# A six-layer decoder pipeline: its pass cut at other places, and the top-k mask moved from ScalarE to GpSimd

## What is computed

```
x = x + attn_latent(ln(x))          # 16 heads of 16, k and v from a latent of 64
x = x + head_mixing(ln(x), ctx)     # per token: 16 heads of 64 attend to each other's heads
x = x + depth_ffn(ln(x))            # router takes the best 128 of 256 tokens, FFN 256-1024-256
x = x + sparse_attn(ln(x))          # softmax over scores that keep their top 25 of 256, others 0
x = x + cross_attn(ln(x), ctx)      # 16 heads of 16, keys beyond a length masked
x = x + ternary_linear(ln(x))
```

## Time and profile before

| | us |
|---|---|
| median of three runs | 6784.98 |
| the profiled execution, its own time | 6756.82 |
| its span from the first to the last instruction | 6755.0 |
| TensorE matmul busy | 5896.7 |
| VectorE busy | 4510.2 |
| ScalarE busy | 4012.6 |
| GpSimd busy | 1507.3 |

### The profile page before, as it was taken

The page is one execution under the profiler, slowest core; times in us unless marked ns, Lnnn a source line. Parts: engine busy times, 40 slices in busy tenths (PEclk is TensorE's granted clock), DMA queues, the critical chain, the costliest instruction groups (busy, mean ns, idle before and its releaser), DMA issues. The chain is left out here.

```text
span 6755.0 us, 109667 instructions
## 1 busy us (share of the span) xinstructions
PE 5896.7 (87%) x37509; PEld 3877.2 (57%) x37762; DVE 4510.2 (67%) x16186; ACT 4012.6 (59%) x9761; POOL 1507.3 (22%) x2564
## 2 busy tenths in 40 slices
PE   6888988988988988898888898888898898898876
PEld 3565565565565565565565565566556556556542
DVE  1366766666777666776676676666776666677653
ACT  2465666565666665666656566656566655566632
POOL 0122222222222222222222222222222222222211
PEclk7789989899999899999999899999998999999965
DMA  2000000000000000000000000000000000000000
GB/s 79 4 6 6 4 8 6 8 8 6 4 8 7 6 8 6 4 8 8 6 8 6 6 6 8 6 8 7 7 4 8 6 8 8 6 4 8 4 2 5
DMA packets 29456, 54.18 MB, mean 8 GB/s; under 512 B 8145, under 2 KB 9810, under 8 KB 27986
## 3 DMA queue, kind: packets, MB, share of 16 engines
q1 hardware_dynamic: 28770, 45.73, 2.1%
HBM read 37.33 MB, written 8.39 MB: 7 GB/s over the span
## 5 line engine op out<-in xcount | busy, mean ns | idle before, releaser
L914 POOL TENSOR_TENSOR t_pr<-t_pr,sc 128x512 f32<-128x512 f32 x512 | 649.6, 1269 | 1495.9 <-ACT t_pr L839 1495.9
L350 DVE TENSOR_REDUCE m_nm<-bankM 128x2 f32<-128x512 f32 x1024 | 657.0, 683 | 347.9 <-PE bankM L340 344.0
L887 DVE MATCH_REPLACE8 wk<-m,wk 128x256 f32<-128x256 f32 x2048 | 821.0, 408 | 0.0
L340 PE MATMUL bankM<-m_kT,m_q 32*128 32x256 f32 x4096 | 698.5, 466 | 75.4 <-DVE m_nm L350 74.3
L883 DVE MAX8 m<-wk 128x8 f32<-128x256 f32 x2048 | 759.2, 412 | 0.0
L651 ACT ACTIVATE xk_area<-bankH,xb 64x256 f32<-64x256 f32 x1024 | 480.7, 469 | 460.4 <-PE bankH L546 438.1
L394 PE MATMUL bankM<-m_q,m_kT 32*128 32x512 f32 x2048 | 627.9, 691 | 0.0
L883 DVE MAX8 m<-sc 128x8 f32<-128x256 f32 x1024 | 380.0, 412 | 327.5 <-ACT sc L830 290.1
L340 PEld LDWEIGHTS bankM<-m_kT,m_q 32*128 32x128 f32 x4096 | 411.3, 216 | 312.4 <-DVE m_nm L350 133.6
L845 ACT ACTIVATE t_pr<-t_pr,t_nm 128x256 f32<-128x256 f32 x1024 | 463.9, 504 | 182.5 <-POOL t_pr L914 180.5
L408 ACT ACTIVATE m_pT<-bankM,keymask 128x512 f32<-128x512 f32 x512 | 323.7, 683 | 247.4 <-PE bankM L394 247.4
(11 more groups left out here) (207 smaller groups left out, 12011.2 us busy)
## 6 DMA issues: line engine op xcount, KB each, us to landing
xin<-x_in SPq DMA_DIRECT2D x32, 256.0 KB, 2.6
ctxA<-ctx_in SPq DMA_DIRECT2D x32, 256.0 KB, 2.6
ctxB<-ctx_in SPq DMA_DIRECT2D x32, 256.0 KB, 3.5
out<-x SPq DMA_DIRECT2D x32, 256.0 KB, 2.0
w<-w_w SPq DMA_DIRECT2D x2, 1024.0 KB
xwq<-w_xwq SPq DMA_DIRECT2D x1, 1024.0 KB
xwk<-w_xwk SPq DMA_DIRECT2D x1, 1024.0 KB
xwv<-w_xwv SPq DMA_DIRECT2D x1, 1024.0 KB
```

The source lines that it names most:

```text
L340: last = nc.tensor.matmul(bank[x][:, j * S:(j + 1) * S], b["q2"][r:r + 32, e, j, t * P:(t + 1) * P], b["kT"][r:r + 32, e, :], start=not ma ...
L350: nc.vector.tensor_reduce(b["nm"][:, i % 2, 2 * (i // 2) + x, :], banks[u % 3][:].rearrange("p (j s) -> p j s", j=2), AX.X, ALU.max, negat ...
L887: m = nc.vector.match_replace(out=wk[:, k, t, :], in_to_replace=take, in_values=src[:, t, :], imm_value=-BIG)
L914: nc.gpsimd.tensor_tensor(sp_[:, u % 2], taken[:, u % 2], sc[:, u % 3], ALU.mult).then_inc(g["sp_mul"], 1)
```

## The change

**The pass is cut elsewhere.** h is split into h1 (up to the last `xot`) and h2 (from the `xwo` projection on), t into t1 (LayerNorm, projections, the first eight heads that it takes) and t2 (the other eight, the output projection and the sum). A pass now runs m and h1 of element i+2, h2 and t1 of i+1, t2 and c of i. The letters of the new table are m, g (h2), u (t2), h (h1), t (t1), c. It puts m, h2 and t2 ahead of h1, t1 and c on every engine.

**Waits.** LayerNorm 1 of h1 and the start of c wait for m's result (`mla_x`); the first projection of h1 waits for the end of h2 (`md_x3`); t1's k projection and `x3b` wait for the end of t2 (`spa_x`), its LayerNorm for `md_x3`; c's LayerNorm waits for `spa_x`. m waits for nothing of c any more. Semaphores of t go on counting from t2 to t1 within a pass; a pass that has t1 and no t2 adds t2's counts by hand (`T2_COUNTS`).

**SyncE.** `ctxA` is loaded at the start of the pass, `xin` of the next pass after LayerNorm 1, and the wait for the stored x stands at the start of the next pass.

**The mask.** `taken` is made by GpSimd as `wk == -BIG` (L944 of the new kernel), with 128x512 elements for each of the 512 heads; ScalarE's Relu is gone.

**The passes.** Ahead of the loop: m; h1; m, h1, h2 and t1. Behind it: one pass of all six with no further x to load; h2, t2, t1 and c; t2 and c. The number of passes stays 35.

```diff
     "pool": runs("""
-        t h c m t h t h t h c2 t10 h t2 h c t3 h t h t h t3 h t3 h t h t2 c2 t3 c t m2 t2 h3 t6 m t10"""),
+        m g u c m2 u4 g2 u4 g h u8 m u16 t4 c2 h3 t16 h2 c h t4 h t4 h2 t4 h t4 h c3"""),
...
+        def tensor_h1(pe):
             for k in range(12):
...
+                if k == 0:
+                    pe.wait_ge(g["ctxA_in"], 16)
+                    if mode["h2"]:
+                        pe.wait_ge(g["md_x3"], 2)
...
+        def tensor_h2(pe):
+            yield
             for t in range(NT):
                 for jp in range(QUADS):
...
+        def tensor_t2(pe):
+            b = bufT
+            yield from tensor_heads(pe, 0)
+            yield from at_out_pe1(pe, "spa", b, bankT, HALF)
...
+        def tensor_t1(pe):
             yield from ln_pe(pe, 3, lnT, bankT[0])
...
+            yield from tensor_heads(pe, HALF)
...
-                yield
-                act.wait_ge(g["sp_top"], u + 1)
-                if u >= 2:
-                    act.wait_ge(g["spa_tr"], u - 1)
-                nc.scalar.activation(taken[:, u % 2].rearrange("p t s -> p (t s)"), wk[:, u % 2].rearrange("p t s -> p (t s)"),
-                                     ACT.Relu, bias=-1.0, scale=-2.0 / BIG).then_inc(g["sp_tk"], 1)
...
+                if u >= first + 2:
+                    pool.wait_ge(g["spa_tr"], u - 1)
+                nc.gpsimd.tensor_scalar(taken[:, u % 2], wk[:, u % 2], -BIG, 1.0, ALU.is_equal, ALU.mult).then_inc(g["sp_tk"], 1)
...
-            if mode["c"]:
-                pe.wait_ge(g["lin_o"], 1)
...
-            yield from ln_act(act, 0, lnM, bankM[0], free=g["lin_y"] if mode["c"] else None)
+            yield from ln_act(act, 0, lnM, bankM[0])
...
-        one_pass(m=0, loaded=True)
+        one_pass(m=0)
         setup_rest()
-        one_pass(m=1, h=0)
-        one_pass(m=2, h=1, t=0)
+        one_pass(h1=0, more=1)
+        one_pass(m=1, h1=1, h2=True, t1=True, more=2)
         with nc.Fori(0, nb - 3) as i:
-            one_pass(m=i + 3, h=i + 2, t=i + 1, c=i)
-        one_pass(h=nb - 1, t=nb - 2, c=nb - 3)
-        one_pass(t=nb - 1, c=nb - 2)
-        one_pass(c=nb - 1)
+            one_pass(m=i + 2, h1=i + 2, h2=True, t2=True, t1=True, c=i, more=i + 3)
+        one_pass(m=nb - 1, h1=nb - 1, h2=True, t2=True, t1=True, c=nb - 3)
+        one_pass(h2=True, t2=True, t1=True, c=nb - 2)
+        one_pass(t2=True, c=nb - 1)
```

More of the change, by code:

```diff
@@ L793, in tensor_t, with raw @@
             project_N(bankT[0], lnT["xT"], w["swv"], g["spa_v"])
+            yield from tensor_heads(pe, HALF)
+        def raw(act, u, first):
             yield
[L795 to L799, removed]
-                    yield
[L801 to L808, removed]
@@ L841, in scalar_t, with scalar_heads @@
+            act.wait_ge(g["spa_s"], u + 1)
+            if u >= first + 3:
+                act.wait_ge(g["sp_mul"], u - 2)
+            nc.scalar.activation(sc[:, u % 3].rearrange("p t s -> p (t s)"), bankT[u % 2][:], ACT.Copy).then_inc(g["sp_sc"], 1)
+        def scalar_heads(act, first):
+            b = bufT
+            for u in range(first, first + 3):
+                yield from raw(act, u, first)
+            for u in range(first, first + H // 2):
                 yield
@@ L892, in vector_t, with vector_t2, vector_t1, pool_heads @@
                     src = wk[:, k]
-            yield from at_out_dve(dve, "spa", b, bankT)
+        def vector_t2(dve, link):
+            yield from vector_heads(dve, 0, link)
+            yield from at_out_dve(dve, "spa", bufT, bankT)
             yield
-            dve.wait_ge(g["sp_xb"], 1)
-            if mode["c"]:
-                dve.wait_ge(g["stored"], 16)
+            dve.wait_ge(g["len_in"], 16)
             add_rows(dve, x4, bankT[1], x3b, g["spa_y"], g["spa_x"])
-        def pool_t(pool):
+        def vector_t1(dve, link):
             b = bufT
-            yield from ln_pool(pool, 3, lnT)
             yield
-            nc.gpsimd.tensor_tensor(x3b[:], xa[:], w["sbo"][:].unsqueeze(1).broadcast_to([P, NT, D]), ALU.add).then_inc(g["sp_xb"], 1)
-            for u in range(H):
+            dve.wait_ge(g["md_x3"], 2)
+            yield from ln_dve(dve, 3, xa, lnT)
+            yield
+            if mode["t2"]:
+                dve.wait_ge(g["spa_ont"], 1)
+            ln_dve2(dve, 3, xa, lnT)
+            yield
+            dve.wait_ge(g["spa_v"], 1)
+            nc.vector.tensor_tensor(b["va"][:, :, :, 0:HD], bankT[0][:].rearrange("p (t h c) -> p t h c", t=NT, c=HD),
+                                    w["sbv"][:].rearrange("p (h c) -> p h c", c=HD).unsqueeze(1).broadcast_to([P, NT, H, HD]),
+                                    ALU.add).then_inc(g["spa_va"], 1)
+            yield from vector_heads(dve, H // 2, link)
+        def pool_heads(pool, first):
+            b = bufT
+            for u in range(first, first + H // 2):
                 yield
@@ L914, in pool_t, with pool_t2, pool_t1 @@
                 nc.gpsimd.tensor_tensor(sp_[:, u % 2], taken[:, u % 2], sc[:, u % 3], ALU.mult).then_inc(g["sp_mul"], 1)
+        def pool_t2(pool):
+            yield from pool_heads(pool, 0)
+        def pool_t1(pool):
+            yield from ln_pool(pool, 3, lnT)
+            yield
+            pool.wait_ge(g["md_x3"], 2)
+            if mode["t2"]:
+                pool.wait_ge(g["spa_x"], 1)
+            nc.gpsimd.tensor_tensor(x3b[:], xa[:], w["sbo"][:].unsqueeze(1).broadcast_to([P, NT, D]), ALU.add).then_inc(g["sp_xb"], 1)
+            yield from pool_heads(pool, H // 2)
         def tensor_at(pe, n, masked):
@@ L1123, in _ @@
+                    if t1 and not t2:
+                        for n, units in T2_COUNTS.items():
+                            sp.sem_inc(g[n], units)
+                    if more is not None:
+                        sp.wait_ge(g["hm_xb"], 1)
+                        sp.wait_ge(g["ln1_xn"], 2)
+                        sp.dma_start(xin[:], x_in[more]).then_inc(g["x_in"], 16)
                     if c is not None:
                         sp.wait_ge(g["lin_o"], 1)
-                        sp.dma_start(out[c], x4[:]).then_inc(g["stored"], 16)
@@ L1126, in _ @@
-                        sp.wait_ge(g["stored"], 16)
+                        sp.dma_start(out[c], x4[:]).then_inc(s_stored, 16)
+                        if not t1:
+                            sp.wait_ge(s_stored, 16)
+                    if more is not None:
+                        sp.wait_ge(g["x_in"], 16)
                 @block.tensor
                 def _(pe):
-                    woven("pe", pe, streams(t=tensor_t(pe), h=tensor_h(pe), c=tensor_c(pe), m=tensor_m(pe)))
+                    woven("pe", pe, present(m=tensor_m(pe), h2=tensor_h2(pe), h1=tensor_h1(pe),
+                                          t2=tensor_t2(pe), t1=tensor_t1(pe), c=tensor_c(pe)))
```

178 lines of the change are left out of this document (95 added, 83 removed).

## The result

The changed kernel takes 7277.8 us (median of 4 runs, 7269.5 to 7280.0), the kernel before 6784.0 in the same session: a ratio of 1.073, 95% interval 1.069 to 1.077. It is slower by 494 us, where 143 us faster was forecast; the time lies 378 us above the range.

A forecast was written before the change was run, and what follows sets the result against it. TensorE was taken to pace both halves of the old pass, VectorE the new m half. 82.3 + 107.0 + 6.2 + 0.8 = 196.3 us per pass; 378.6 + 5889 + 346 = 6614, plus 28: 6642 us, range 6450 to 6900.

The forecast's parts named there:

- X: Half of a pass where h1, t1 and c work: 119.6 us before, forecast to become 107.0.
- the mask's ends: Last head of each half, where GpSimd's longer mask shows: 0.4 us twice, 0.8 us per pass.
- the three heads, `xwo`, the `xwv` records and the end: Changes to the h1, t1, c half: heads -5.0 us, `xwo` -5.0, `xwv` records behind the barrier -6.6, uncovered end +4.0.
- rival 2: TensorE's clock stays up where m starts: some 6 us per pass go, 6462 us in all; chance 0.17.
- Y: Half of a pass where m, h2 and t2 work: 75.0 us before, forecast 82.3, paced by VectorE.
- rival 1: VectorE and a new TensorE wait at the first `xwv` projection stretch m's half to 90.3 us; 6882 us; chance 0.25.
- I take 10 us as used: In m's half, three added heads (17.3 us of VectorE) fill 10 of its 11.7 free us.
- The comparison: GpSimd's mask of 128x512 per head: taken as 1.0 us, between 0.22 and 1.27.
- Replacements untouched: VectorE's top-k replacements, 396 to 419 ns, are not lengthened by GpSimd's added work; 0 us counted.
- The barrier: Change of pass, moved to another place in the cycle: stays at 6.2 us per pass.
- rival 3: Nothing but a rotation: TensorE keeps its shares, the barrier its cost; 200.5 us per pass, 6768 us; chance 0.12.
- the sign that the prediction named for rival 3: Sign against the forecast: a pass whose idle time on TensorE is again 22 us.

The follow-up runs named there:

- experiment 2: Changed kernel with GpSimd's comparison as one operation (is_equal alone, without the multiplication by 1.0): 7060.7 us, ratio 1.048 to the kernel before.
- experiment 3: Changed kernel without the comparison; GpSimd multiplies the scores by ones, so every key counts: 6912.7 us, ratio 1.022 to the kernel before.
- experiment 7: Changed kernel with both the one-operation comparison and c's mask-row matmuls ahead of its first scores issued twice: 6982.4 us, ratio 1.032 to the kernel before.
- experiment 1: Kernel before the change with only its mask moved from ScalarE to GpSimd's two-operation comparison: 6766.2 us, ratio 1.002 to the kernel before.
- experiment 4: Changed kernel, filled: c's mask-row matmuls ahead of its first scores issued twice, 16 more per pass: 6973.0 us, ratio 1.033 to the kernel before.
- experiment 5: Changed kernel with the row-selecting matmuls in c's second scores issued twice, 16 more per pass: 7018.7 us, ratio 1.039 to the kernel before.
- experiment 6: Changed kernel with both c's mask-row matmuls and c's row-selecting matmuls issued twice: 6975.9 us, ratio 1.031 to the kernel before.
- experiment 8: Changed kernel with one-operation comparison, c's mask-row matmuls twice, and 16 more such matmuls in m's first scores: 7194.7 us, ratio 1.063 to the kernel before.

## Why the prediction was wrong

By its own terms, one pass: forecast 196.3, measured 218.4, 22.1 more.

- **X: 107.0 and 0.8 for the mask's ends, measured 121.1.** What failed is what the sum has no term for: **it took over the clock of the old pass.** The half X from which 119.6 us were read had 13.7 us at the lower level, the changed kernel's has 41.0; the 27.3 us more are worth 11.2 of the 13.3 that are missing, at 0.41. In the better passes of experiment 2, X is 202.2 - 90.7 - 6.2 = 105.3, with 6.8 us at the lower level, so some 108 at the old half's clock. So the three heads, `xwo`, the `xwv` records and the end were sized right together. Over the whole run the lower level grew by 946 us, at 0.41 some 390 of the 636 us by which the forecast is off. The prediction knew that the clock could change with the order (rival 2) and let it change in one direction only. It looked at the one place where the old pass was low, m's start at 0.57, and not at where the new order might put another. The row that could have warned is the spread: passes of the kernel before differ by up to 10 us (197 to 207), with 20 to 44 us of the lower level, and so held the price too. A mean of 200.8 hides that.
- **Y: 82.3, measured 91.2.** This was the term behind rival 1, whose 90.3 is nearly met. Up to `md_x3` Y took 68.5 us where 64.7 was worked out, and VectorE's free time there is 6.0 us: of 11.7 it used 5.7, not 10 and not 2. The step "I take 10 us as used" is what failed. Part of it is TensorE's wait for the ranks (L759), 1.1 us per pass more than without the comparison: the prediction knew that short VectorE instructions beside GpSimd can last longer, and counted 0. The other 5 us lie behind `md_x3`: 22.7 us where the sum kept the old 17.6. The first 16 `xwv` records (3.72 us, at 2193.83) now run there, on TensorE, which is busy 19.6 of 22.7 us. The prediction saved their 6.6 us in X and charged the half that moved into m's tail to nobody. Of rival 1, VectorE's share came true in part; its new wait did not, since TensorE found work at hand and did not stand at that projection. That its price is nearly met is in part luck.
- **The comparison: 1.0 us, measured 1.94,** outside the bounds of 0.22 and 1.27. The nearest row was a multiplication with a broadcast column; two operations on one full input cost nearly twice that, and one operation 1.51. The estimate of 0.77 us from the Trainium skill (GPSIMD Engine Reference, section 3.1) is further off still. By experiment 3 the comparison costs some 2 us in Y, where 0.8 was counted for the whole pass. Through the clock it can cost more: one operation less took 205 us off the changed kernel (experiment 2) and nothing off the filled one (experiment 7).
- **Replacements untouched: right in all runs but one.** In the changed kernel's profiled execution their mean is 420 ns and the maximum 505, where they kept to 396 to 419 before. But it is 405 to 409 in experiments 1 to 7, with the same comparison in the same pass among them (4 to 6), so neither the comparison nor the order makes it; the cause is open. VectorE's 51 us more busy time do come with the comparison in the new pass: it is 36 to 53 us in all such runs, 6 without a comparison (experiment 3), 5 in the old pass (experiment 1). L759 carries 28 of the 51. For L759 the rule of the Trainium skill on the shared port pair (SBUF — State Buffer, Who interferes with whom), that the second of the two is shut out for the whole instruction of the first, agrees with the trace: GpSimd's multiplication ends at 2156.42, and the 0.28 us of L759 later, at 2156.70, VectorE is done. No replacement shows such a stop.
- **The barrier** (5.61 us of standing), the head (374.4 for 378.6) and the last passes (365 for 346) were right or near. So was "nothing but the ends" for the comparison on the old pass, as experiment 1 shows.

The terms add up: Y + 8.9, X + 13.3, together 22.2 of 22.1. The forecast's own range doesn't follow from the bounds that it names: Y of 80.6 and an end of 2 give 6531 us, Y of 86 and an end of 7 give 6843 and not 6745, so it reached past the kernel before. At equal time of the lower clock the new pass is still 3 to 4 us longer than the old one. The best pass seen in any run of the new order took 201.6 us, so even rival 3's 200.5 was not reached. Work that left X came back in Y: TensorE is busy 60.9 + 19.6 = 80.5 us there, where the old half Y had 68.0 and 78 were forecast. The forecast needed TensorE's idle time to fall from some 22 us per pass to 17; it is 24.7, the sign that the prediction named for rival 3.

Not settled: which property of the pass decides whether the clock comes up at the second unit or at the seventh. Of two passes with the same instructions, one does and the other doesn't. Where all of the 3 to 4 us at equal clock stand isn't settled either. A mask on ScalarE in the new pass was not tried.

## What to carry to other kernels

TensorE's granted clock is a term of the sum, with a sign open in both directions: before a pass is reordered, sum the time at each level per pass, look at how far passes of the same instructions differ, and let the range take in that spread on either side. Work moved to where an engine "has room" is free only if the trace shows idle time of that engine at that very place (16 `xwv` records behind `md_x3` did not find it here); each piece saved in one half must appear in the other. When a kernel gets slower with TensorE busier and its instruction count unchanged, read the durations of one matmul in two passes (here 1.13 and 2.08 us for four) ahead of any wait.

## What the runs showed of the hardware

TensorE's clock stayed at its lower level of 1.2 GHz for 37.5 us with TensorE busy 36.7 of 37.6 us. A third of that is matmuls that use 32 of 128 rows (L395); the rest are matmuls with 72 and 128 rows and transposes. The kind of work doesn't decide alone: in experiment 2 the same units ran at 2.4 GHz in the neighbouring pass. The Trainium skill (TensorE: Matmul & The Clock Gate, Part 1, on the clock's two states) ties the higher level to TensorE being busy; these 37.5 us don't agree with that. It puts the penalty of the ramp at under 1% of a typical kernel's span; here the kernel spent 2318 of 7274 us low, at 0.41 some 13% of its span, and 16 more matmuls per pass made it 4% faster (experiment 4 against the changed kernel). Passes repeat their clock pattern: nearly all alike in the changed kernel, mostly in turn of two in experiment 2, and in turn of two in experiment 8.

A GpSimd comparison of 128x512 f32 takes 1.94 us with two operations and 1.51 with one. On this kernel it was free in the old pass. A VectorE TENSOR_SCALAR of 128x128 took up to 1.28 us beside a GpSimd multiplication of 128x512, where it takes 0.28 otherwise.
